# Two attention layers and two feed-forward layers on one core: weights of the routed layer and two contexts are loaded ahead of the iterations, the first keys stored there too, with other stages and orders on all engines

## The chip, the core and the metric

The kernel runs on one core of one Trainium2 chip. The metric is the device time in microseconds (us) of one launch, a median of runs.

## The reference, cut to what matters

For x of shape (16, 128, 256) and a context of the same shape, batch by batch:

```python
x = x + _L0_xattn_ref(_layernorm(x), ctx_2048, ctx_2048)   # 16 heads of 16 columns, causal softmax
x = x + _L0_ffn_ref(_layernorm(x), base_w, base_b, router_w, router_b, lora_A, lora_B)
                                                            # dense 256x256 plus two of 8 rank-16 experts by top-2 gates
x = x + _L1_xattn_ref(_layernorm(x), ctx_2048, ctx_2048, gamma)  # the same on 8 heads over columns: 256x256 scores, no mask
x = x + _L1_ffn_ref(_layernorm(x), w1, w2, gamma)           # rms norm, 8-bit activations, ternary weights, 256 -> 1024 -> 256, gelu
```

All is float32. The kernel keeps that precision in the scores by splitting each query and key into three bf16 parts, stacked along the rows of the array.

## The kernel before

**One batch at a time through a pipeline over t.** Each of the five engines has its own in-order program: `iterations` calls a function per iteration t, `fill` for t = 0 to 7, `body` for t = 8 to 15 (14 and 15 as a hardware loop of one turn) and `drain` from 16 to END - 1 = 45. In it every operation is called once, in an order written out by hand, and works on batch b = t - stage, where the stages are the constants at the top of the file (LOAD_KV = 0, ROWS0 = 2, COPY_MAX0 = 4 ...). Engines count t each for themselves and meet only in semaphores; a stage thus says how an operation stands in its own engine's order and not when it runs. An operation whose wait isn't met holds up all behind it on its engine.

**Attention 0 (names ending in 0).** SP loads the context (`load_kv`). GpSimd splits it into the bf16 parts of K (`k_high`, `k_rest_`, `k_mid`, `k_low`), except batch 0, which VectorE splits in `split_k0`. SP stores them to DRAM (`store_k`) and loads them back re-laid by heads (`load_k0`). ScalarE normalises x (`norm0`, `norm0_high`), GpSimd makes the parts (`q0_rest`, `q0_mid`, `q0_low`), TensorE turns them (`turn_q0`), ScalarE copies them (`copy_q0`), SP stores and loads them (`store_q0`, `load_q0`). TensorE computes the scores a first time (`scores0`, four groups), VectorE takes row maxima and splits them (`maxima0`, `split_max0`, `split_max0_low`), TensorE turns them (`turn_max0`), ScalarE copies them (`copy_max0`), SP writes them into two further rows of the query tile with two transfers of 4 KB (`rows0`). Then TensorE computes the scores transposed and with the maximum taken off (`scores0_t`), ScalarE exponentiates (`exp0`), TensorE multiplies by V (`pv0`), ScalarE copies the sums (`copy_u0`), TensorE turns them (`turn_u0`), VectorE divides and adds (`rz0_`, `a0_`, `x1_`).

**Routed layer.** `stats1_`, `mv1_`, `rstd1_`, `norm1`, `turn_xh1`, `copy_xh1`, `ff` (two float32 products of 392 columns, L1256), then `logits_`, `top_`, `gap_`, `exp2`, the gates, `gated_`, `turn_gated`, `copy_gated`, `lora` (L1273), `moe_out`.

**Attention 1** runs the same way (names ending in 1; `load_k1`, `load_q1`, `rows1`), some five iterations later. **The last layer** (`xn_`, `amax_in`, `round_in`, `quant_in`, `turn_in`, `up`, `gelu`, `amax_hid`, `round_hid`, `quant_hid`, `turn_hid`, `copy_hid`, `down`, `scale_output`, `add_output`) runs in `drain` alone.

**Queues.** All loads and stores of contexts, keys, queries and rows go through SP's queue in program order. x in groups and all weights go through ScalarE's. In `fill` SP's order of an iteration is rows1, load_kv, store_k, load_v1, load_q0, rows0, load_k0, store_q1, load_k1, load_q1, store_q0. `load_q0` and `load_k0` of batch b wait for the last `scores0_t` of batch b - 2, `load_kv` of b for K's split of b - 1 and for `place_v0` of b - 2.

## Time and profile before

| | us |
|---|---|
| median of 3 runs | 413.86 |
| lowest, highest | 408.65, 415.42 |
| the profiled execution | 415.81 |
| its span in the trace | 413.4 |
| granted TensorE clock, mean | 0.93 |

The span is the time between the first and the last instruction of the trace; 2.4 us of the profiled execution lie around it. PE is TensorE's matmuls, PEld its weight loads, DVE VectorE, ACT ScalarE, POOL GpSimd. SPq and ACTq are the queue of an engine (its sequencer), where transfers are issued. A row with DMA in the chain of waits runs from the issue of a transfer to its landing.

### The profile page before, as it was taken

To read this page: it belongs to the slowest core of one execution; us is meant where nothing else is said; L and a number is where in the kernel's file an instruction comes from. 1 tells how busy PE (TensorE), PEld (TensorE's weight loads), DVE (VectorE), ACT (ScalarE), POOL (GpSimd) and SP (SyncE) were. 2 spreads that over 40 slices of the span, in tenths; PEclk is the share of its full clock that TensorE was granted. 3 is DMA by queue.
4 is the path that set the end of the run, shared out by engine and by line. 5 is a ranking of instruction groups with operands and counts; after the bars stand their busy time and mean duration, and the time that the engine had idled before them with its cause. 6 is when DMAs were issued, how large, how long until landed. Compare 5 with 4: busy or idle time off the path is not lost.

```text
span 413.4 us, 9678 instructions
## 1 busy us (share of the span) xinstructions
PE 318.2 (77%) x3010; PEld 192.7 (47%) x3010; DVE 307.9 (74%) x838; ACT 264.4 (64%) x501; POOL 230.9 (56%) x449
## 2 busy tenths in 40 slices
PE   0047366497799899999999999999787578566883
PEld 0024244264465465665655665665443234234453
DVE  6432362759899687889997978897885574999983
ACT  2124153355577488789777876777465347988993
POOL 6257465838585557769656676235424113566534
PEclk9996796888899899999999999999996789999999
DMA  3675774976655738658757577623413400001111
GB/s 101 203 210 131 223 212 105 271 204 168 169 152 172 219 86 237 187 167 225 201 159 212 147 209 193 166 57 92 108 57 94 90 2 1 2 17 36 39 52 63
DMA packets 73137, 56.20 MB, mean 136 GB/s; under 512 B 5376, under 2 KB 62592, under 8 KB 73088
## 3 DMA queue, kind: packets, MB, share of 16 engines
q1 hardware_dynamic: 68896, 50.87, 44.8%
q10 hardware_dynamic: 4192, 4.73, 4.5%
q8 instruction: 24, 0.39, 0.5%
q14 instruction: 25, 0.20, 0.2%
HBM read 36.45 MB, written 18.87 MB: 134 GB/s over the span
## 4 chain that ended last, share of the span: by engine, by line
PE 45%; DMA 16%; DVE 12%; issue 9%; ACT 8%; SPq 6%; POOL 3%; ACTq 0%; POOLq 0%; DVEq 0%
DMA q<-max_t 8%; PE ps_u L1186 6%; PE ps_st L1155 6%; PE ps_s L1140 5%; DMA k<-k_parts 5%; PE ps_ff L1256 4%; PE ps_st L1122 3%; PE ps_st L1126 3%; PE ps_u L1169 3%; DVE max L1801 3%; PE ps_s L1104 2%; PE ps_t L1284 2%; PE ps_s L1108 2%; SPq L616 2%; DMA k_parts<-k_split 2%
## 5 line engine op out<-in xcount | busy, mean ns | idle before, releaser
L1801 DVE TENSOR_REDUCE max<-ps_s 128x2 f32<-128x512 f32 (+1 forms) x192 | 127.1, 685 | 49.0 <-PE ps_s L1108 28.0
L1507 ACT ACTIVATE p<-ps_st 128x512 f32<-128x512 f32 x128 | 71.9, 596 | 23.6 <-PE ps_st L1155 15.6
L1497 ACT ACTIVATE p<-ps_st 128x512 f32<-128x512 f32 x64 | 37.2, 597 | 30.3 <-PE ps_st L1126 29.9
L1140 PE MATMUL ps_s<-k,q 96*128 96x256 bf16 x256 | 51.2, 284 | 5.6 <-DMA k<-k_parts 3.2
L1155 PE MATMUL ps_st<-q,k 98*128 98x256 bf16 x256 | 48.0, 288 | 4.9 <-ACT p L1507 3.1
L1186 PE MATMUL ps_u<-p,v 128*32 128x256 f32 x512 | 39.5, 422 | 3.4 <-POOL v L874 3.4
L1122 PE MATMUL ps_st<-mask_k,ident_bf 128*128 128x512 bf16 x64 | 26.9, 421 | 18.3 <-DMA q<-max_t 17.5
L1155 PEld LDWEIGHTS ps_st<-q,k 98*128 98x128 bf16 x256 | 21.8, 102 | 20.9 <-issue 6.4
L1140 PEld LDWEIGHTS ps_s<-k,q 96*128 96x128 bf16 x256 | 20.3, 100 | 22.8 <-issue 10.9
L923 POOL TENSOR_SCALAR var<-mv 128x1 f32<-128x1 f32 x32 | 7.3, 229 | 41.8 <-DVE mv L1890 34.1
L1284 PE MATMUL ps_t<-ident_bf,q_split 128*128 128x128 bf16 x128 | 12.8, 259 | 21.6 <-POOL q_split L897 21.6
L817 POOL TENSOR_SCALAR k_split<-kv_in 128x1024 bf16<-128x1024 f32 x15 | 15.7, 1049 | 24.2 <-DMA k_parts<-k_split 20.1
L1256 PE MATMUL ps_ff<-wff_sb,xh_t 128*128 128x392 f32 x64 | 27.5, 556 | 2.0 <-DVE w_mean L2048 1.6
L1126 PE MATMUL ps_st<-q,k 98*128 98x128 bf16 x256 | 27.3, 233 | 0.0
L1104 PE MATMUL ps_s<-mask_q,ident_bf 128*128 128x512 bf16 x64 | 25.7, 401 | 1.7 <-DMA k<-k_parts 1.7
L1126 PEld LDWEIGHTS ps_st<-q,k 98*128 98x128 bf16 x256 | 21.7, 105 | 11.1 <-issue 3.5
L1511 ACT ACTIVATE xh<-xs,shift,rstd 128x256 f32<-128x256 f32 x32 | 19.2, 601 | 11.9 <-POOL shift L926 7.8
L1108 PE MATMUL ps_s<-k,q 96*128 96x128 bf16 x256 | 26.0, 226 | 0.0
L1568 ACT COPY q_t<-ps_t 128x1024 bf16<-128x1024 bf16 x16 | 16.1, 1006 | 15.1 <-PE ps_t L1284 15.1
L1169 PE MATMUL ps_u<-p,v 128*32 128x128 f32 x512 | 25.5, 292 | 0.0
L1027 POOL TENSOR_SCALAR amax_c<-amax,rms 128x1 f32<-128x1 f32 x16 | 4.9, 307 | 36.6 <-DVE amax L2203 35.9
L1108 PEld LDWEIGHTS ps_s<-k,q 96*128 96x128 bf16 x256 | 20.7, 101 | 8.7 <-issue 1.4
(147 smaller groups left out, 798.3 us busy)
## 6 DMA issues: line engine op xcount, KB each, us to landing
k_parts<-k_split SPq DMA_DIRECT2D x16, 512.0 KB, 4.1
q<-q_parts SPq DMA_DIRECT2D x32, 256.0 KB, 3.8
k<-k_parts SPq DMA_DIRECT2D x32, 256.0 KB, 3.6
kv_in<-in_kv SPq DMA_DIRECT2D x16, 256.0 KB, 3.7
q_parts<-q_t SPq DMA_DIRECT2D x16, 256.0 KB, 3.7
q<-q_parts SPq DMA_DIRECT2D x32, 128.0 KB, 3.9
k<-k_parts SPq DMA_DIRECT2D x32, 128.0 KB, 3.6
q_parts<-q_split SPq DMA_DIRECT2D x16, 256.0 KB, 2.8
```

Of the source, the lines that this page charges most:

```text
L1104: pe.matmul(out_[:, :], ident_bf[:, :], mask_q[:, :, :].rearrange("p g k -> p (g k)"), start=True, stop=False, skip_group_check=True)
L1108: last = pe.matmul(out_[:, j * P:(j + 1) * P], q0[0:STK, odd, c:c + P], k0[0:STK, odd, c:c + P], start=False, stop=(j == G - 1), skip_grou ...
L1122: pe.matmul(out_[:, :], ident_bf[:, :], mask_k[:, :, :].rearrange("p g k -> p (g k)"), start=True, stop=False, skip_group_check=True)
L1126: last = pe.matmul(out_[:, j * P:(j + 1) * P], k0[0:STM, odd, c:c + P], q0[0:STM, odd, c:c + P], start=False, stop=(j == G - 1), skip_grou ...
L1140: last = pe.matmul(out_[:, f * D:(f + 1) * D], q1[0:STK, odd, h * D + f * P:h * D + (f + 1) * P], k1[0:STK, odd, h * D:(h + 1) * D], start ...
L1155: last = pe.matmul(out_[:, f * D:(f + 1) * D], k1[0:STM, odd, h * D + f * P:h * D + (f + 1) * P], q1[0:STM, odd, h * D:(h + 1) * D], start ...
L1169: last = pe.matmul(ps_u[32 * j:32 * j + 32, g * P:(g + 1) * P], v0[:, odd, h, :], p0[:, g, j * P:(j + 1) * P], start=True, stop=True, skip ...
L1186: last = pe.matmul(ps_u[32 * j:32 * j + 32, g * D:(g + 1) * D], v1[:, f * H1 + h, :], p1[:, h, f * D:(f + 1) * D], start=(f == first), sto ...
L1256: last = pe.matmul(ps_ff[:, 0:NFF], xh1_t[:, f, :], wff_sb[:, f, :], start=(f == 0), stop=(f == FT - 1), skip_group_check=True)
L1497: act.activation(p0[:, g, :], ps_st[bank_of(ST_BANKS, f"s0t{g}")][:, :], ACT.Exp, scale=SCALE).then_inc(exp0_done[g], 1)
L1507: act.activation(p1[:, h, :], ps_st[bank_of(ST_BANKS, f"s1t{h}")][:, :], ACT.Exp, scale=SCALE).then_inc(exp1_done[h], 1)
L1801: dve.tensor_reduce(out_, src, AX.X, ALU.max, negate=True).then_inc(done, 1)
```

## The change

1. **Ahead of the iterations**: SP loads both context 0 and context 1, waits for `split_k0`, and stores the keys of batch 0 (`send_k(0)`). ScalarE's queue issues the third group of x, base_b, w_ff in two transfers, router_b and lora_b. Before, context 1 and keys 0 stood in SP's iteration 1 behind `store_q0` of batch 0, and the weights in ScalarE's iteration 2. The two gammas go to iteration 3. One semaphore for six weights becomes three (`base_b_in`, `w_ff_in`, `lora_in`). Groups 4 and 5 of x and w1, w2 are loaded one iteration later, and the sums over w1 and w2 are taken one later (`W_BATCH` 10 - FF; `weight_sum(0)` at the end of t = 7, `stats0_group(5)` of t = 8, `weight_sum(1)` of t = 9).
2. **Orders in fill**: on TensorE `turn_gated`, `lora` and `turn_q0` stand before `scores0_t`, `ff` and all four `pv0` before `turn_max0`. On SP `load_k0` stands before `rows0`. On ScalarE `copy_max0` follows `exp2` and `copy_u0`, and `copy_gated` and `copy_q0` follow at once, before `exp0`. On GpSimd `k_rest_` and `k_mid` go ahead of `rstd1_`, and `q1_rest` stands between `k_high` and `q0_low`.
3. **Orders in body**: SP's `rows1` is first, before `load_kv`. ScalarE's `norm2` goes before `copy_max0`. Orders of `pv0`, `pv1` and of some DVE operations are exchanged.
4. **Drain and stages**: `xn_` 17 to 16, `rms_` 17 to 18, `quant_in` 20 to 21, `copy_hid` 27 to 28, `down` 28 to 29, `scale_output` 30 to 31, `add_output` 29 to 31, `dequant_in` 20 to 23, `dequant_hid` 27 to 30, END one more. On DVE `copy_hid` stands before `amax_hid`; on TensorE `down` is first and `up` and `turn_hid` go ahead of the last groups.
5. **Waits**: `norm0` and `norm2` wait for `q0_rest` (`q1_rest`) of the batch before, no longer for its `q0_low` (`q1_low`).

```diff
-X_ITERATIONS = {0: 2, 1: 3, 3: 4, 5: 5}
-W_LOADS = {4: 0, 6: 1}
-W_BATCH = 9 - FF
+X_ITERATIONS = {1: 3, 4: 4, 6: 5}
+GAMMAS = 3
+W_LOADS = {5: 0, 7: 1}
+W_BATCH = 10 - FF
...
             load_x(sp, 0)
             load_x(sp, 1)
+            sp.dma_start(kv_in[:, 0, :, :], kv[0]).then_inc(kv0_landed, 16)
+            sp.dma_start(kv_in[:, 1, :, :], kv[1]).then_inc(kv_landed, 16)
+            sp.wait_ge(k_split_step, 4)
+            send_k(0)
             iterations(sp, fill, body, drain)
...
             def fill(t, odd):
-                rows1(t, odd)
                 load_kv(t, odd)
                 store_k(t)
+                rows1(t, odd)
+                load_q0(t, odd)
+                load_k0(t, odd)
+                rows0(t, odd)
+                store_q1(t)
+                load_k1(t, odd)
                 load_v1(t, odd)
-                load_q0(t, odd)
-                rows0(t, odd)
-                load_k0(t, odd)
-                store_q1(t)
-                load_k1(t, odd)
                 load_q1(t, odd)
                 store_q0(t)
...
-                act.wait_ge(q0_split_step, b * 3)
+                if later(b, 1):
+                    act.wait_ge(q0_split_step, b * 3 - 2)
...
             act.activation(warm[:, :], warm[:, :], ACT.Exp)
+            load_x(act, 2)
+            act.dma_start(base_b_all[:, :], base_b.partition_broadcast(P)).then_inc(base_b_in, 16)
+            for f in range(FT):
+                act.dma_start(wff_sb[:, f, :], w_ff[f * P:(f + 1) * P, :]).then_inc(w_ff_in, 16)
+            act.dma_start(router_b_all[:, :], router_b.partition_broadcast(P)).then_inc(w_ff_in, 16)
+            act.dma_start(lora_b_sb[:, :], lora_b).then_inc(lora_in, 16)
             iterations(act, fill, body, drain)
```

TensorE's and ScalarE's orders in `fill` are new throughout; as they stand after the change, cut behind `turn_max0` and `exp0(t, 0)`:

```python
def fill(t, odd):
    scores1_t(t, odd, 6)
    turn_back(t)
    scores1(t, odd, 6)
    scores1(t, odd, 2)
    scores1(t, odd, 0)
    turn_u0(t)
    scores1(t, odd, 1)
    turn_gated(t)
    scores1_t(t, odd, 1)
    scores1(t, odd, 3)
    lora(t)
    pv1(t, 0, 0)
    turn_q0(t)
    scores1(t, odd, 7)
    scores0_t(t, odd, 1)
    scores0_t(t, odd, 2)
    scores1(t, odd, 4)
    scores0(t, odd, 2)
    pv1(t, 1, 0)
    scores0(t, odd, 3)
    scores1_t(t, odd, 2)
    scores0_t(t, odd, 0)
    turn_max1(t)
    scores0_t(t, odd, 3)
    scores0(t, odd, 0)
    turn_xh1(t)
    scores0(t, odd, 1)
    turn_u1(t)
    pv0(t, odd, 1)
    pv1(t, 0, 1)
    ff(t)
    pv0(t, odd, 2)
    pv0(t, odd, 3)
    pv0(t, odd, 0)
...
    turn_max0(t)
...
def fill(t, odd):
    norm2_high(t)
    exp1(t, 0)
    exp1(t, 7)
    norm2(t)
    exp2(t)
    copy_u0(t)
    copy_max0(t)
    copy_gated(t)
    copy_q0(t)
    norm0(t)
    exp1(t, 5)
    exp0(t, 1)
    exp0(t, 2)
    norm1(t)
    copy_max1(t)
    exp0(t, 3)
    exp1(t, 2)
    exp1(t, 4)
    copy_xh1(t)
    norm0_high(t)
    copy_u1(t)
    exp0(t, 0)
```

## Rows read from the trace of the kernel before

**Rows 1.** The page: busy time by engine, and the granted clock in 40 slices.

```profile
PE 318.2 (77%) x3010; PEld 192.7 (47%) x3010; DVE 307.9 (74%) x838; ACT 264.4 (64%) x501; POOL 230.9 (56%) x449
...
PEclk9996796888899899999999999999996789999999
```

**Rows 2.** The page's transfers: tiles, queue, count, KB each, median us to landing.

```profile
k_parts<-k_split SPq DMA_DIRECT2D x16, 512.0 KB, 4.1
...
q_parts<-q_t SPq DMA_DIRECT2D x16, 256.0 KB, 3.7
```

**Rows 3.** Timeline of SP's queue in fill: start, us, queue and line, transfer.

```profile
11.87 0.33 SPq L664 DMA_DIRECT2D q_parts<-q_t  x1
12.24 0.43 SPq L634 DMA_DIRECT2D kv_in<-in_kv  x1
...
30.43 1.23 SPq L728 DMA_DIRECT2D q<-max_t  x2
...
43.43 1.46 SPq L728 DMA_DIRECT2D q<-max_t  x2
...
57.79 1.43 SPq L728 DMA_DIRECT2D q<-max_t  x2
...
74.92 1.28 SPq L728 DMA_DIRECT2D q<-max_t  x2
```

**Rows 4.** The chain that ended last, 0 to 125 us: start, us, what.

```profile
12.79 7.96 DMA k_parts<-k_split
...
21.48 3.45 DMA k<-k_parts
...
31.07 2.70 DMA q<-max_t
...
44.30 5.13 DMA q<-max_t
...
51.37 0.85 PE ps_t L1284 x8
...
58.40 6.85 DMA q<-max_t
...
68.61 1.09 PE ps_ff L1273 x2
...
75.54 6.40 DMA q<-max_t
...
123.80 2.19 DVE w_sum L2040
```

**Rows 5.** Timeline of ACT around one copy_max0 in fill.

```profile
57.51 0.26 ACT L1576 COPY max_t<-ps_t 32x128 bf16<-32x128 bf16 x1 [0.35 <-PE ps_t L1230]
...
57.91 0.20 ACT L1615 ACTIVATE e<-gap 128x1 f32<-128x1 f32 x1
...
58.01 0.57 ACT L1592 COPY u<-ps_u 128x512 f32<-128x512 f32 x1
```

**Rows 6.** Waits: engine and line, for whom, us in total, times, longest.

```profile
POOL k_split L817 <- DMA k_parts<-k_split: 20.1, 5, 7.1
```

**Rows 7.** Windows: us, busy time and count by engine, granted clock, DMA share, GB/s.

```profile
60.00:62.00 2.00, 0.33 (x1) 0.14 (x1) 1.25 (x5) 0.27 (x1) 1.75 (x4) 1.00 1.15 281
...
160.00:180.00 20.00, 19.94 (x216) 11.91 (x215) 16.41 (x51) 16.07 (x34) 13.94 (x24) 1.00 0.70 198
```

**Rows 8.** Timeline of the last layer: two xn, two amax_hid, the last down.

```profile
374.00 0.46 DVE L2195 SCALAR_TENSOR_TENSOR xn<-xs,mv,mlp_gamma_all 128x256 f32<-128x256 f32 x1
...
378.02 0.46 DVE L2195 SCALAR_TENSOR_TENSOR xn<-xs,mv,mlp_gamma_all 128x256 f32<-128x256 f32 x1
...
393.72 1.22 DVE L2221 TENSOR_REDUCE amax<-hid 128x1 f32<-128x1024 f32 x1 [0.44 <-ACT hid L1736]
...
396.64 1.22 DVE L2221 TENSOR_REDUCE amax<-hid 128x1 f32<-128x1024 f32 x1 [0.43 <-ACT hid L1736]
...
408.87 1.05 PE L1434 MATMUL ps_ff<-w_q,hq_t 128*128 128x256 bf16 x8 [0.79 <-DVE hq_t L2258]
```

446 lines of the change are left out of this document (222 added, 224 removed).

## The prediction, made before the changed kernel was run

> **What bounds the kernel now.** I read the page first. TensorE is busiest, 318.2 of 413.4 us, and the slices show where it is not: the granted clock drops in the first quarter and again late, and is at its upper level, 2.4 GHz, for most of the middle [rows 1]. The windows split the span in four. The fill (to about 125 us) has idle engines everywhere; between 60 and 62 us TensorE works 0.33 of 2 us, while the 16 DMA engines are busy throughout [rows 7]. The middle (to about 250 us) is TensorE's: 19.94 of 20 us at full clock [rows 7]. Next comes the end of the attention layers (to 351 us), then the last layer alone, on VectorE and ScalarE.
>
> I then followed the chain of waits through the fill, with SP's queue beside it. It goes round one ring per iteration: `rows0` issues two small transfers, they land, `scores0_t`, `turn_q0`, `pv0`, `lora`, the next `scores0` and `ff` run, the maxima are turned and copied, the next `rows0` issues. `rows0` stands at 30.43, 43.43, 57.79 and 74.92 us: rings of 13.0, 14.4 and 17.1 us [rows 3]. Steady iterations take about 15.6 us of TensorE's work. The transfers of these rings (the second of two) landed in 2.70, 5.13, 6.85 and 6.40 us [rows 4]. They carry 4 KB, so the three long ones waited behind larger ones.
>
> **The change, part by part.** *Keys 0 and context 1 ahead.* Before, `store_k` of batch 0 was issued at 12.79 us, behind `store_q0` and `load_kv` (11.87, 12.24) [rows 3], landed after 7.96 us beside the weights, and its keys 3.45 us after the last issue, so that the first scores could begin at 24.93 [rows 4]. Now the store goes out when VectorE has split (about 7.4 us there, 1 to 2 later if the early loads slow context 0) and has landed before `store_q0`. `store_q0` at 11.87, plus 3.7 [rows 2], plus four issues of 0.6 us, plus 3.45, gives 21.3. I take a start 3.1 us earlier at `rows0` (bounds 1.5 and 4.5: the split late, or all of the difference).
>
> *Landing of `rows0`.* Before, `store_q0`, `load_kv`, `store_k` (1 MB) and 384 KB of `load_q0` are issued in the 5 us ahead of it. Now `turn_q0` doesn't follow `scores0_t` and `copy_q0` follows `copy_max0`, so those stores come behind `rows0`, and about 10 us remain until the next. Against that, `load_k0` (384 KB, two issues) goes ahead of it; those loads are issued once the last `scores0_t` is out, some 4 us before the maxima are copied, so SP is free by then. I take 3.3 us, near the one unhindered row (2.70) and above it for what still overlaps: 1.8, 3.5 and 3.1 less, 8.4 in all. Bounds: nothing (the queues stay full) and 10.3 (2.70 each).
>
> *What leaves the ring.* `turn_q0` (0.85 us at the low clock, five rings) and `lora` (1.09, two rings) [rows 4] run while `rows0` is in flight: 4.3 + 2.2 us. `pv0` of group 1 moves behind the scores to the full clock: 1. Bounds 4 and 9 (the ring has other members where ScalarE was last).
>
> *What enters it.* `copy_max0` now waits for `exp2` (0.20) and `copy_u0` (0.57) and thus for all `pv0`, where before it came ahead of both [rows 5]. With two hand-overs and two more `pv0` groups of about 0.36 that is up to 1.9 per ring; the path through the maxima (1.3 + 0.85 us after the last scores) hides about half. I take 0.9 over five rings: 4.5 (bounds 2 and 9.5).
>
> Sum of the fill: -3.1 - 8.4 - 4.3 - 2.2 - 1.0 + 4.5 = -14.5. Walking the new orders by hand from the start, with row durations, I come to `rows0` at 39 instead of 43.4, 52 instead of 57.8 and 65 instead of 74.9. From t = 5 `copy_gated` stands before `copy_q0`, the attention-1 traffic joins, and 768 KB of x come one iteration later, so I give 2.5 back: **-12**.
>
> *Weight sums.* `weight_sum(0)` stood in VectorE's wait at t = 6 and now ends t = 7; `weight_sum(1)`, 2.19 us on the chain [rows 4], only moves to t = 9; six batches of x statistics go from the end of t = 7 to that of 8. One more sum is exposed: **+2.2** (bounds 0 and 4.5, the statistics too).
>
> *Body.* TensorE has no idle time to give, so the orders bring little. `rows1` goes out ahead of `load_kv` (0.43 us of issue [rows 3]), where its landing was at times the last thing waited for; `norm2` goes before `copy_max0` (0.6 us). The looser waits of `norm0` and `norm2` are free: those norms run behind longer queues. I take **-1** (bounds -3 and +3).
>
> *Drain and last layer.* There VectorE sets an iteration of 4.02 us (`xn_` at 374.00 and 378.02), and from about 385 us ScalarE one of 2.92 (`amax_hid` at 393.72 and 396.64), with 0.43 us of idle VectorE [rows 8]. `xn_` one iteration earlier and `copy_hid` one later take 0.46 and 0.68 us out of the VectorE-bound stretch. The end pays: `copy_hid` of batch 15 must now wait for `down` of 14, which waits for `copy_hid` of 14, all behind `quant_hid` of 15, where before `quant_hid` of 15 was followed by its turn (0.61), its copy (0.68) and its `down` (1.05 [rows 8]). That is 0.68 + 1.05 in place of the turn, +1.2 with the hand-over. Together **+0.2** (bounds -1.5 and +3).
>
> Total: -12 + 2.2 - 1 + 0.2 = -10.6, so the span goes from 413.4 to 402.8 and the profiled execution from 415.81 to 405.2, a ratio of 0.9745. The profiled execution stood 0.5% above the median of 413.86, so against that median the forecast is 403.3; I say **403.5**.
>
> **The clock.** About four of the eight score groups of an iteration run at 1.2 GHz in the rings above (0.85 us each in the timeline, 0.45 at 2.4), behind 4 to 5 us in which TensorE was idle: the slices with 6 and 7 [rows 1]. `turn_gated`, `lora` and `turn_q0` now fall in that gap. My sum keeps the low clock. If the gap were filled well enough, 1.6 us per ring, 8 us over five, would come on top: 395.5. The trace gives no case in which two short bursts held the clock up, so that is a rival of small chance. The Trainium skill (TensorE: Matmul & The Clock Gate, The HAM clock gate) says that activity releases the throttle and idleness restores it; the trace agrees, as the clock falls in every such wait. By it the 395.5 would come if what is now in the gap counts as activity, and the 403.5 if it doesn't.
>
> **The rivals.**
>
> *A. The landing doesn't get shorter (chance 0.22).* In 60 to 62 us the engines were busy at over 100% of the window at 281 GB/s [rows 7], and `load_k0` now adds 384 KB right ahead of `rows0`. For: all queues end in the same transfer engines. Against: the 1 MB of stores is gone from ahead of it. Then -8.4 becomes 0 or -1, the fill about -4.5, and the time 411. The Trainium skill (DMA: Bandwidth & Descriptors, Issuing engines are not separate DMA queues) states that transfers issued by different engines run on the same 16 DMA engines and interleave, and that issuing from several saves issue time alone. By it the early weights slow context 0 and the first term would be its 1.5; no row shows the two loads side by side.
>
> *B. The fill's gain is lost in the body (0.12).* TensorE is full [rows 7], so an earlier start carries through only if batches aren't held by VectorE, which takes both the sum and the statistics in t = 7 to 9. If `norm2` before `copy_max0` costs its 0.6 us in each of some 14 later iterations, 8.4 us go: 412.
>
> *C. The clock stays up (0.08).* 395.5, as above.
>
> *D. Slower: the ring of keys becomes the bound (0.07).* Now TensorE must pass `turn_q0` before `scores0_t`, `turn_q0` of b needs `q0_low` of b, which stands behind `k_high` of b on GpSimd, and that waits until `store_k` of b - 1 has landed. GpSimd waited 20.1 us in 5 times for this, once 7.1 [rows 6]. By my walk the store is issued 8 us after `ff`, lands 4.1 later [rows 2], and GpSimd needs 2 to 3 more (14 to 15 in all); the turn is wanted at 18.4, a ring of 12.8 later and 5.6 on, when `rows0` has landed. From a landing of about 8 us on, the fill's iterations grow. With 8 of landing, 8.6 of GpSimd's work (its longest stretch from one `k_high` to its `k_low`) and 3 of turn, copy and issue they take 19.6 instead of the 17.1 of the longest ring: six give +15, less 3 for the start, +2 from the rest: 428. At half that excess 421, about where "slower" begins. Queued behind on TensorE would be `scores0_t` and all after it.
>
> *E. Nothing moves (0.05)*: the ring is re-formed by ScalarE (`copy_gated` before `copy_q0` waits for a chain of gates of 3 to 4 us), 413.
>
> The forecast itself has 0.46 and the range 397 to 408.
>
> **How the numbers follow.** Faster by over 2% means below 405.6, slower above 422.1, about what a measurement of this kernel can tell from no change (its three runs span 1.6%). Faster: 0.35 of the forecast's 0.46, all of C (0.08), and 0.07 of A and B, where no more than half of their loss comes: 0.50. Slower: 0.05 of D and 0.02 of B at its bounds: 0.07. The same: 0.43. Eight in ten lie between 393, which reaches past C, and 415, past A, B and E, which leaves out D and the tails.
>
> **What would show it.** First `scores0` at 21 to 22.5 us; `rows0` near 27, 39, 52 and 65; the second of its transfers landing in about 3.3 us; `turn_q0` ahead of `scores0_t` with no wait on it for GpSimd; the chain in the fill without `turn_q0` and `lora`; the body at 15.6 us an iteration; weight sums on the chain twice; about 60 us from the last `out_` to the end, as now. Landings of 5 to 7 us mean A, waits of TensorE for `q_split` mean D, waits of `copy_q0` for `turn_gated` mean E.

## The result, and the profile after

The changed kernel takes 416.47 us (median of 20 runs) where the kernel before takes 414.37 (20 runs), a ratio of 1.0088 with a 95% interval of 1.0044 to 1.0131. It is a little slower, where 403.5 was forecast. Ratios here and below compare undisturbed runs only, so they differ a little from the quotient of two medians.

The profiled execution has a span of 414.9 us, 1.5 more than before. The page after, as in [rows 1]:

```profile
PE 323.6 (78%) x3010; PEld 197.7 (48%) x3010; DVE 316.3 (76%) x838; ACT 264.8 (64%) x501; POOL 234.7 (57%) x449
...
PEclk9999787896899999999999999999887688699999
```

TensorE and VectorE do the same instructions in more time (323.6 and 316.3 us instead of 318.2 and 307.9). Marks in the timelines divide the 1.5 us:

| us in the span | before | after | difference |
|---|---|---|---|
| `copy_max0` of b = 0 | 30.1 | 26.6 | -3.5 |
| `copy_max0` of b = 4 | 92.4 | 86.2 | -6.2 |
| `copy_max0` of b = 5 | 108.7 | 105.8 | -2.9 |
| last `out_` (attention layers end) | 351.6 | 348.6 | -3.0 |
| from last `out_` to the end | 61.8 | 66.3 | +4.5 |

`copy_max0` of b = 0 is the copy of the row maxima of batch 0. So a gain is made in the fill, half of it is gone by the sixth batch (b = 5), and the last layer takes more than what is left.

**The start.** The chain of waits and, behind it, SP's queue (the lines to set beside [rows 3, 4]):

```profile
1.63 6.17 DMA kv_in<-in_kv
...
23.65 4.70 DMA k_parts<-k_split
...
30.38 2.88 DMA q<-max_t
```

```profile
26.58 0.26 ACT L1589 COPY max_t<-ps_t 32x128 bf16<-32x128 bf16 x1 [3.19 <-PE ps_t L1239]
...
28.43 0.58 SPq L619 DMA_DIRECT2D k<-k_parts  x1
29.06 0.62 SPq L620 DMA_DIRECT2D k<-k_parts  x1
29.73 0.61 SPq L733 DMA_DIRECT2D q<-max_t  x1
```

Context 0 is issued at 1.63 us, as before, but lands after 6.17 us, before the change after 3.1: `base_b`, `w_ff`, `router_b` and context 1 were issued between 1.4 and 2.9 us and `lora_b` at 4.8 (x[2] went out at 0.9 us before the change too). That they share the transfer engines with it is borne out below, where it lands after 3.2 us without them. Batch 0's keys are therefore stored at 11.01 us, not 7.4. Its maxima are copied at 26.58 all the same, 3.5 us earlier than before. But SP stands at `load_k0` of batch 1, which waits for a store issued at 23.65 and landed at 28.4, and `rows0` is queued behind it: it goes out at 29.73, 0.7 us earlier than before. The chain of waits runs from the late context 0 through VectorE's and GpSimd's work on the parts to this store.

**The rings.** `rows0` stands at 29.73, 42.79, 58.16, 72.68, 87.05 and 106.06 us. The chain from 54 us on, at the third of them and after:

```profile
57.96 1.08 DVE pick L1954
...
59.86 0.49 PE ps_t L1275
...
60.37 0.27 ACT gated_t L1635
...
60.69 1.22 PE ps_ff L1284 x2
61.91 0.85 PE ps_t L1295 x8
62.77 0.58 PE ps_st L1131
```

The gates are computed (`pick`), turned and copied (`gated_t`), then `lora` and `turn_q0` run, and only then the first `scores0_t` (62.77), 4.6 us after `rows0` was issued. The landing is not on this chain, but it ends within 0.1 us of it: the second transfer was issued at 58.8 and took 3.9 us. In the fourth ring `turn_q0` is done first and TensorE waits 1.2 us for the landing.

The clock takes its part of each ring. In the second ring the scores begin at 47.42 us, 2.1 earlier than before. The score groups (a product with the mask, then four with the keys) after the change, and the first rows of the same ring before it:

```profile
47.42 0.61 PE ps_st L1131
...
51.87 0.43 PE ps_st L1131
...
52.72 0.38 PE ps_s L1113
```

```profile
49.48 0.61 PE ps_st L1122
...
52.69 0.32 PE ps_st L1122
```

After the change the first rows at the upper level come at about the same time as before, and more groups have run at the lower one. In rings one to four, 23 of 32 groups start at the lower level (7, 7, 5 and 4 of eight), before 10 (4, 2, 2 and 2). At 0.85 us a group instead of 0.45 that is an estimate of up to 5 us. Three other profiles with the same fill have 18 (fill_only), 21 (body_pe) and 25 (body_act).

At the fifth ring it is a queue again:

```profile
74.27 3.09 DMA q_parts<-q_split
...
81.02 4.66 DMA k_parts<-k_split
...
87.65 7.07 DMA q<-max_t
```

`load_q1` waits for the store of batch 0's second queries, `store_q0` and `store_k` stand behind it, `load_k0` behind the landing of that, and the 4 KB of `rows0` then take 7.07 us. Before the change that landing took 1.8 us. It is where 3.3 of the 6.2 us go.

**The windows**, for [rows 7]:

```profile
60.00:62.00 2.00, 1.65 (x6) 0.98 (x7) 1.22 (x5) 0.27 (x1) 0.23 (x1) 0.50 0.69 100
160.00:180.00 20.00, 19.24 (x212) 12.69 (x210) 16.69 (x46) 17.76 (x34) 13.58 (x23) 1.00 0.67 182
```

The gap is filled now (1.65 of 2 us instead of 0.33), but at a granted clock of 0.50, the lower level. In the middle TensorE is no longer full: 19.24 of 20 us. Its waits there, in 140 to 330 us (for what, us in total, times, longest):

```profile
PE ps_st L1164 <- DMA q<-max_t: 2.9, 5, 1.2
PE ps_st L1131 <- DMA q<-max_t: 2.3, 4, 1.2
```

Nine waits for landings of maxima, 5.2 us; the kernel before has two, 0.9 us together, in the same stretch.

**The last layer** (beside [rows 8]). First its start, then a stretch from 372 us and one from 387 us:

```profile
349.85 1.87 PE L1418 MATMUL ps_s<-w_q,xq_t 128*128 128x512 bf16 x4 [1.25 <-ACT hid L1744]
...
353.65 1.87 PE L1418 MATMUL ps_s<-w_q,xq_t 128*128 128x512 bf16 x4 [1.72 <-ACT hid L1744]
```

```profile
372.31 0.72 POOL L1071 TENSOR_TENSOR xs<-y,xs 128x256 f32<-128x256 f32 x1
...
372.50 1.08 DVE L2263 TENSOR_SCALAR hq<-hr 128x1024 bf16<-128x1024 f32 x1
```

```profile
387.33 0.68 DVE L2263 TENSOR_SCALAR hq<-hr 128x1024 bf16<-128x1024 f32 x1
387.49 0.58 POOL L1053 TENSOR_SCALAR amax_c<-amax 128x1 f32<-128x1 f32 x1 [1.33 <-DVE amax L2235]
...
388.04 0.72 POOL L1071 TENSOR_TENSOR xs<-y,xs 128x256 f32<-128x256 f32 x1
...
388.11 0.16 DVE L2254 RECIPROCAL qscale<-amax_c 128x1 f32<-128x1 f32 x1
388.19 0.72 DVE L2247 TENSOR_SCALAR xq<-xr 128x256 bf16<-128x256 f32 x1
...
388.31 1.24 ACT L1754 ACTIVATE hr<-hid,round_all,qscale 128x1024 f32<-128x1024 f32 x1 [0.23 <-DVE qscale L2254]
```

At the start three `up`s, of the second to the fourth batch, take 1.87 us at the lower clock, where those of the kernel before take 1.02, and the first three iterations take 3.8, 3.8 and 5.3 us instead of 2.9, 3.4 and 4.0. Later, instructions of VectorE and GpSimd that touch take longer. VectorE's `quant_hid` takes 1.08 us instead of 0.68 beside GpSimd's `add_output` (the rows at 372 us), and `xq` 0.72 or 0.75 instead of 0.28. From 387 us on `keep_amax_hid` on GpSimd (one number a partition, 0.21 to 0.23 us in all but one batch of the kernel before) takes 0.58 beside `quant_hid` in four batches, and two iterations take 3.24 us instead of 2.92. From the first `amax_hid` to the last it is 53.8 us, before 49.7, and this is where it goes:

| us between `amax_hid` of | before | after | copy_between | up_late | two_lines |
|---|---|---|---|---|---|
| b = 0 and 3 | 10.3 | 12.9 | 11.4 | 10.3 | 9.7 |
| b = 3 and 5 | 8.0 | 8.0 | 8.0 | 8.0 | 8.0 |
| b = 5 and 9 | 13.8 | 15.5 | 14.4 | 15.5 | 14.4 |
| b = 9 and 15 | 17.6 | 17.4 | 17.4 | 17.1 | 17.5 |

The last three columns are experiments that come below. The loss lies in the first three iterations (2.6 us) and between b = 5 and 9 (1.8). The two iterations of 3.24 us cost nothing in the end, since the four behind them take 2.60 to 2.89.

### The profile page after: what moved, and what is told of

The parts are those of the page before. It is cut to its first block, busy times and chain, and to the rows that moved or that the text cites. A ratio compares the mean times of both kernels' runs of the same rounds, so it can differ in the third digit from the quotient of the medians.

```text
span 414.9 us, 9679 instructions
## 1 busy us (share of the span) xinstructions
PE 323.6 (78%) x3010; PEld 197.7 (48%) x3010; DVE 316.3 (76%) x838; ACT 264.8 (64%) x501; POOL 234.7 (57%) x449
## 4 chain that ended last, share of the span: by engine, by line
PE 26%; DMA 18%; issue 16%; DVE 13%; POOL 12%; SPq 10%; ACT 3%; POOLq 0%; ACTq 0%; DVEq 0%
DMA q<-max_t 10%; DVE max L1815 4%; PE ps_u L1195 4%; DMA k_parts<-k_split 4%; SPq L620 3%; PE ps_st L1164 3%; PE ps_s L1149 3%; PE ps_st L1131 3%; POOL xs L1071 3%; PE ps_st L1135 3%; SPq L619 2%; DMA q_parts<-q_t 2%; SPq L742 2%; PE ps_s L1418 2%; DMA kv_in<-in_kv 1%
## 5 line engine op out<-in xcount | busy, mean ns | idle before, releaser
L1195 PE MATMUL ps_u<-p,v 128*32 128x256 f32 x512 | 38.3, 423 | 3.6 <-POOL v L883 3.6
L1131 PE MATMUL ps_st<-mask_k,ident_bf 128*128 128x512 bf16 x64 | 28.6, 447 | 13.7 <-DMA q<-max_t 13.6
L932 POOL TENSOR_SCALAR var<-mv 128x1 f32<-128x1 f32 x32 | 9.4, 294 | 51.0 <-DVE mv L1904 34.9
L1164 PEld LDWEIGHTS ps_st<-q,k 98*128 98x128 bf16 x256 | 21.8, 102 | 21.4 <-DMA q<-max_t 7.7
L1149 PEld LDWEIGHTS ps_s<-k,q 96*128 96x128 bf16 x256 | 19.8, 99 | 24.7 <-issue 16.1
L1295 PE MATMUL ps_t<-ident_bf,q_split 128*128 128x128 bf16 x128 | 11.5, 241 | 23.0 <-POOL q_split L906 23.0
L1135 PE MATMUL ps_st<-q,k 98*128 98x128 bf16 x256 | 28.7, 242 | 0.0
L1135 PEld LDWEIGHTS ps_st<-q,k 98*128 98x128 bf16 x256 | 22.9, 110 | 11.4 <-issue 4.7
L1117 PE MATMUL ps_s<-k,q 96*128 96x128 bf16 x256 | 28.3, 240 | 0.0
L1113 PE MATMUL ps_s<-mask_q,ident_bf 128*128 128x512 bf16 x64 | 28.3, 442 | 0.0
L1117 PEld LDWEIGHTS ps_s<-k,q 96*128 96x128 bf16 x256 | 22.8, 109 | 10.6 <-issue 4.4
L1522 ACT ACTIVATE q_split<-xs,shift,rstd 128x256 bf16<-128x256 f32 (+1 forms) x32 | 22.6, 706 | 7.6 <-POOL shift L935 7.5
L1265 PE MATMUL ps_ff<-wff_sb,xh_t 128*128 128x392 f32 x64 | 26.6, 541 | 0.8 <-ACT xh_t L1621 0.5
L1418 PE MATMUL ps_s<-w_q,xq_t 128*128 128x512 bf16 x64 | 18.9, 423 | 10.4 <-ACT hid L1744 10.4
```

The source lines that it names most:

```text
L1113: pe.matmul(out_[:, :], ident_bf[:, :], mask_q[:, :, :].rearrange("p g k -> p (g k)"), start=True, stop=False, skip_group_check=True)
L1117: last = pe.matmul(out_[:, j * P:(j + 1) * P], q0[0:STK, odd, c:c + P], k0[0:STK, odd, c:c + P], start=False, stop=(j == G - 1), skip_grou ...
L1131: pe.matmul(out_[:, :], ident_bf[:, :], mask_k[:, :, :].rearrange("p g k -> p (g k)"), start=True, stop=False, skip_group_check=True)
L1135: last = pe.matmul(out_[:, j * P:(j + 1) * P], k0[0:STM, odd, c:c + P], q0[0:STM, odd, c:c + P], start=False, stop=(j == G - 1), skip_grou ...
L1149: last = pe.matmul(out_[:, f * D:(f + 1) * D], q1[0:STK, odd, h * D + f * P:h * D + (f + 1) * P], k1[0:STK, odd, h * D:(h + 1) * D], start ...
L1164: last = pe.matmul(out_[:, f * D:(f + 1) * D], k1[0:STM, odd, h * D + f * P:h * D + (f + 1) * P], q1[0:STM, odd, h * D:(h + 1) * D], start ...
```

## The experiments

My theory after the two profiles: the early loads eat the lead of the first keys; the fill's new orders still gain; the last layer's orders lose about 4 us, by the slow `up` and by the meeting of VectorE and GpSimd; the body loses, by `norm2` in front of `copy_max0` (rival B). The rival theory: one thing is at fault, the start, and the rest is scatter. Kernels of one group ran side by side with the kernel before, so that ratios, not medians, are to be compared across groups. The medians are of 6 to 12 runs, those of before of 11 to 29.

| kernel | median | before | ratio [95%] |
|---|---|---|---|
| u_drain | 414.37 | 413.07 | 1.0005 [0.9956, 1.0054] |
| u_body | 415.18 | 413.07 | 1.0022 [0.9981, 1.0062] |
| u_fill | 420.84 | 413.07 | 1.0138 [1.0071, 1.0205] |
| u_weights | 416.44 | 413.07 | 0.9971 [0.9901, 1.0040] |
| clear_start | 416.83 | 415.19 | 1.0031 [0.9989, 1.0072] |
| all_three | 410.66 | 415.19 | 0.9849 [0.9792, 0.9906] |
| copy_between | 416.64 | 415.19 | 0.9978 [0.9933, 1.0022] |
| up_late | 416.01 | 415.19 | 1.0034 [0.9990, 1.0078] |
| fill_only | 409.63 | 412.21 | 0.9901 [0.9851, 0.9951] |
| rows_first | 406.64 | 412.21 | 0.9892 [0.9847, 0.9937] |
| max_first | 417.82 | 412.21 | 1.0169 [1.0109, 1.0229] |
| lead_alone | 412.41 | 412.21 | 0.9978 [0.9930, 1.0026] |
| body_act | 409.40 | 414.31 | 0.9883 [0.9838, 0.9927] |
| body_dve | 409.52 | 414.31 | 0.9909 [0.9872, 0.9946] |
| body_pe | 414.50 | 414.31 | 0.9972 [0.9920, 1.0024] |
| body_sp_pool | 415.08 | 414.31 | none given |
| two_lines | 416.50 | 413.60 | 1.0108 [1.0056, 1.0160] |
| weights_t1 | 407.67 | 413.60 | 0.9831 [0.9771, 0.9890] |

### Undoing one part at a time

**u_drain**: the stages and orders of `drain` as before.

```
-COPY_HID = 28        +COPY_HID = 27
-DOWN = 29            +DOWN = 28
 (and the other stages, and def drain of all five engines)
```

> The changed kernel, with the stages of the last layer and all five drain orders of the kernel before; lead-in, fill and body stay changed. Theory (the new order of the last layer costs 4 to 5 us): from the last out_ to the end it takes 62 us again instead of 66, and the time falls by about 4.5 us against the changed kernel, to a ratio of 0.998 against before. Rival (the last layer only pays for work that the attention part got rid of, 3 us there): the end falls by 4.5, the attention part grows by 3, ratio 1.005.

From the first `amax_hid` to the last it is 49.7 us again, and the span is 410.4. In the eleven profiles with the drain of before it is 49.6 to 49.7 us, in the six with the change's drain 53.8 to 53.9: the last layer does cost 4.2 us. The time is 0.8% below that of the change, with intervals that just overlap.

**u_body**: `def body` of all engines as before.

> The changed kernel with the body orders of before on all engines; the places of the weight work stay. Theory (the body lost 3 us of the fill's 6 through its new orders): 3 us faster than the changed kernel, ratio 1.002. Rival (it lost them through the statistics and the sums that moved into t = 8 and 9): no difference, 1.009.

0.7% below the change, again with intervals that just overlap. The profile alone would have said less (span 413.2 against 414.9).

**u_fill**: the fill's orders, and the iterations of the x and weight loads, as before; the start, the body and the drain are the change's.

> The changed kernel, with the fill orders of before on all engines and before's times for x, w1, w2 and the sums over weights; the lead-in (early context 1, keys 0 and weights), body and drain stay changed. Theory (the new fill orders are worth 5 us at t = 7 and the body gives half of it back): 2 to 3 us slower than the changed kernel, ratio 1.015. Rival (what the fill gains is lost in the body, whatever it was): no difference, 1.009.

Slower than the change, by 0.5% with overlapping intervals; the span is 2.6 us longer (417.5 against 414.9). The new fill orders seem to be worth something; nothing shows that they cost.

**fill_only** undoes drain and body together:

> The changed kernel with the body's orders, the last layer's stages and the last layer's orders of the kernel before; the start with its early loads and the fill's orders are those of the change. It differs from all_three by the start alone. If the early loads cost 3 us at the start that nothing gives back, it lies 2 to 4 us above all_three, at 412.5 to 414.5. If the chain of the fill swallows the start, it lies within 1 us of all_three, 410 to 411.5.

1.9% below the change, intervals apart, and 1% below the kernel before. Against all_three (below) it lies 0.5% higher, about 2 us, with intervals that overlap, so which of its two outcomes holds is not decided. The accounts of the parts add up to within 0.4% (0.8 + 0.7). fill_only also differs from u_drain by the body alone (1.0%) and from u_body by the drain alone (1.2%), with intervals apart in both. The six kernels with the new fill that have neither the new drain nor TensorE's, SP's or GpSimd's new body lie at 0.983 to 0.991, all others with the new fill at 0.997 to 1.017.

### The start

**u_weights** and **clear_start** take the early loads out of context 0's way:

```
+                if t == 2:
+                    act.dma_start(base_b_all[:, :], ...).then_inc(base_b_in, 16)
+                    ... w_ff, router_b, lora_b
-            load_x(act, 2)                      # clear_start only; back in t = 0
             sp.wait_ge(k_split_step, 4)
             send_k(0)
+            sp.dma_start(kv_in[:, 1, :, :], kv[1])...   # clear_start only; was ahead of the wait
```

> The changed kernel, but base_b, w_ff, router_b and lora_b are issued at the end of ScalarE's iteration 2 again instead of ahead of the iterations. Theory (they share the transfer engines with context 0, which landed after 6.2 us instead of 3.0): context 0 lands in 3 to 4 us, rows0 of batch 0 stands at 27 us instead of 29.7, and 2 us of it last to the end, ratio 1.004. Rival (later waits take it up): rows0 of batch 0 earlier, the end the same, 1.009.

> The changed kernel with its start emptied of everything but x[0], x[1] and kv[0]: the loads of base_b, w_ff, router_b and lora_b stand at the end of ScalarE's iteration t=2, x[2] again in t=0, and kv[1] is issued by SP behind send_k(0). All orders are those of the change. Theory 1 (the early loads share the 16 DMA engines with kv[0], whose landing went from about 3.0 us before to 6.17 us after, and so ate the lead of the first keys): kv[0] lands after 3.0 to 3.5 us, k_split of head group 0 starts at 4.7 to 5.2 us instead of 7.8, store_k(0) is issued at 7.5 to 8.2 us instead of 11.0, the first row maxima are copied at 24 to 25.5 us instead of 26.6, and the time is 3 to 6 us below the changed kernel's, 411 to 413. Rival 2 (the start has slack: the first scores wait for x and the queries, not for the keys): store_k(0) moves, copy_max0(0) stays within 0.7 us of 26.6, time 415 to 417. Rival 3 (kv[1] comes too late behind send_k): iteration 1 starts 2 to 3 us later, and the time is 417 or more.

In u_weights context 0 lands after 3.71 us, the keys of batch 0 are stored at 8.64 and `rows0` goes out at 27.72, 2.0 us earlier than in the change; `copy_max0` of b = 15 is 4.5 us earlier. The ratio, 0.9971, is 1.2% below the change's and lower than the 1.004 expected, but it rests on four runs. So the early weights cost the start 2 us.

In clear_start too the mechanism is there: context 0 lands after 3.2 us, `k_split` starts at 4.90 us, `store_k` of batch 0 goes at 7.53. Yet `copy_max0` of batch 0 is at 28.5, two later than in the change. The chain:

```profile
11.72 3.96 DMA q_parts<-q_t
...
17.88 4.33 DMA k<-k_parts
...
27.04 1.09 DVE max_split L1845
```

```profile
26.93 1.15 POOL L842 TENSOR_TENSOR k_rest<-kv_in,k_split 128x512 f32<-128x512 f32 x1
```

With the keys out of the way, the store of the queries sets the scores, and that lands later (3.96 us; 3.0 in the change, where the weights had gone; here they are issued at about the same time). And one subtraction of 128x16 numbers on VectorE takes 1.09 us instead of 0.17, because GpSimd's `k_rest` started 0.11 us earlier. `copy_max0` of batch 1 is 4.0 us earlier than in the change (38.6), though the ten other profiles with the change's start and fill have it at 40.1 to 42.4; at b = 6 it is 4.5. Then it is lost: b = 6 to 15 takes 153.3 us instead of 149.4. Rival 2's time, without rival 2's cause.

**lead_alone** is the kernel before with nothing but the keys of batch 0 pulled ahead:

```
             load_x(sp, 1)
+            sp.dma_start(kv_in[:, 0, :, :], kv[0]).then_inc(kv0_landed, 16)
+            sp.wait_ge(k_split_step, 4)
+            send_k(0)
+            sp.dma_start(kv_in[:, 1, :, :], kv[1]).then_inc(kv_landed, 16)
             iterations(sp, fill, body, drain)
```

> The kernel before with the first keys alone hoisted: SP issues kv[0] behind x[1], waits for k_split, stores the keys of iteration 0, issues kv[1], and only then enters the iterations. The weights' loads and all orders are those of before. Theory 1 (the store of the first keys, 12.8 us before, sets the first scores): it is issued at 7.5 to 8 us, the first scores and copy_max0(0) come 3 to 4 us earlier (26 to 27 instead of 30.1), and 1.5 to 3 us of it reach the end: 411 to 413. Rival 2 (the first scores are held by the queries of b=0 or by the orders on the engines): copy_max0(0) moves by less than 1 us, time unchanged, 413.5 to 415.5. Rival 3 (later iterations of the fill are paced by the landings of the row maxima and give the lead back): copy_max0(0) is 3 us earlier, copy_max0(4) less than 1 us, time 413 to 415.

```profile
11.92 4.32 DMA q_parts<-q_t
...
18.43 6.42 DMA k<-k_parts
...
30.13 0.26 ACT max_t L1583
```

The store goes 5.1 us earlier (7.74 instead of 12.79), and the maxima are copied at 30.13, exactly as before. The last load of the keys goes out 3.05 us earlier and takes 2.97 us longer than that of [rows 4] (6.42 instead of 3.45): the weights, the queries and the keys are all still in flight between 12 and 25 us, and from 20 to 25 the transfer engines are busy throughout (the DMA share of that window is 1.07). Rival 2. The chain of waits had shown which transfer came last, not that the others were done sooner.

**weights_t1** puts the four weights where ScalarE is done with t = 1, on top of all_three (below):

> all_three with the loads of base_b, w_ff, router_b and lora_b at the end of ScalarE's iteration t=1 instead of t=2. In clear_start ScalarE is done with its work of t=1 at about 8 us, and the DMA engines are 0.63 busy from 8 to 12 us and 0.66 from 12 to 16. If these 0.9 MB fit there, the queries' store (issued at 11.7 us) lands as before after 4 us, the DMA share from 20 to 24 us falls from 1.04 to below 0.8, copy_max0(0) comes at 26 to 27.5 instead of 28.5 us, and the time is 0 to 2 us below all_three (ratio 0.980 to 0.987). If they stand in front of the stores of keys and queries, copy_max0(0) comes at 28.5 to 31 us, and the ratio is 0.987 to 0.995.

They go out at 6.5 to 9.0 us. `copy_max0` of batch 0 stays at 28.4 us, so the expected step is missed; the ratio of 0.9831, within what its theory said, is the lowest of all, not distinguishable from all_three's 0.9849.

### The body

**max_first** is clear_start with one line moved, and tests rival B's cause. The waits it takes away, in clear_start:

```profile
234.00 0.23 PE L1239 MATMUL ps_t<-ident_bf,max_split 128*32 128x128 bf16 x1
...
234.52 0.81 ACT L1522 ACTIVATE q_split<-xs,shift,rstd 128x512 bf16<-128x512 f32 x1 [1.31 <-POOL shift L935]
...
235.73 0.24 ACT L1589 COPY max_t<-ps_t 32x128 bf16<-32x128 bf16 x1
```

```
                 copy_u0(t)
-                norm2(t)
                 copy_max0(t)
+                norm2(t)
```

> clear_start with one line moved: in ScalarE's body order copy_max0 stands ahead of norm2 again, as in the kernel before. In the profiles with the changed body order copy_max0 is issued 0.8 us (b = 6, 7, 9), 2.3 us (b = 10, 11) and 1.5 us (b = 12, 13) after the transpose that it reads, because norm2 ahead of it waits for GpSimd's rstd2; with the body orders of before the waits are 0 to 0.4 us, but one of 1.0. Theory 1 (these waits are on the path from one iteration to the next): they vanish, the time from copy_max0 of b=6 to b=15 falls from 153.3 us (clear_start) to 145 to 149, and the time by 4 to 6 us, to 411 to 413. Rival 2 (the iteration has that much slack, or norm2, now later, delays the second head group by as much): the waits vanish, b=6 to b=15 stays at 149 to 154 and the time within 2 us of clear_start, 415 to 418.

The waits vanish up to b = 11, and in the profile b = 6 to 15 falls from 153.3 to 149.5 us. The kernel is not faster: 1.0169, where clear_start has 1.0031, though from three runs. TensorE still waits 6.5 us in 8 times for landings of maxima. So the waits before `copy_max0` don't explain the body's cost, and my theory of it fell.

So the body was taken apart by engine. Each of the next four is fill_only with `def body` of one engine (SP and GpSimd together) from the change; body_pe also has the change's unit orders of the body.

> fill_only (ratio to the kernel before 0.990) with ScalarE's body order of the change alone: norm2 and norm2_high ahead of and behind copy_max0, copy_q0 ahead of norm0_high, exp0(0) behind copy_max1. Theory (the cost of the body, about 0.7%, comes from what stands in front of copy_max0): copy_max0 waits 0.8 to 2.3 us for rstd2 as in the changed kernel, and the ratio is 0.995 to 1.000. Rival (another engine's order costs it; what max_first says): the waits are there or shorter, and the ratio stays within 0.986 to 0.994.

> fill_only with VectorE's body order of the change alone: stats2 and mv2 stand four to six instructions later, mv2 directly ahead of split_max0, so GpSimd's rstd2 and ScalarE's norm2 start later. Theory (the late mv2 delays norm2, the queries of the second head group and their store, which SP waits for ahead of the next keys): store_q1 is issued 1 to 2 us later in each body iteration, the time from copy_max0 of b=6 to b=15 rises from 144.3 us to 147 or more, and the ratio is 0.995 or more. Rival: b=6 to b=15 within 1.5 us of 144.3 and a ratio of 0.986 to 0.993.

> fill_only with TensorE's body order of the change alone (turn_back behind scores1(2), the pv0 pieces in the order 2, 1, 0, 3, pv1(1, 1) last). A steady iteration is bound by the chain of scores and maxima rather than by these pieces, which only trade places; expected ratio 0.987 to 0.993, b=6 to b=15 within 1 us of 144.3. If it is TensorE's order that costs the 0.7%, the ratio is 0.996 or more and waits of VectorE for ps_ut or ps_t grow.

> fill_only with SP's and GpSimd's body orders of the change. SP issues load_v1 and load_kv behind rows1 instead of load_kv first: where rows1 waits for copy_max1, the next kv and the next keys are issued later. Theory (SP's queue costs it): kv is issued 1 to 4 us later against copy_max0 in the body, k_parts too, b=6 to b=15 rises by 3 us or more, ratio 0.996 or more. Rival (kv has a whole iteration to land): later issue, no change in the periods, ratio 0.986 to 0.993.

ScalarE's and VectorE's orders cost nothing that the time shows (0.9883, 0.9909; fill_only 0.9901), although b = 6 to 15 takes 148.8 and 147.9 us instead of 144.2. In body_act `copy_max0` mostly doesn't wait as its theory needs (0.8 us at b = 10 and 11, where the change has 2.3), so VectorE's late `mv2` has its part in those waits. TensorE's order comes out 0.7% above fill_only, with intervals that overlap. SP's and GpSimd's have no interval: five of the six runs lie between 413.8 and 422.3, one at 407.5. The expectations of body_pe and body_sp_pool put the period at 144.3 and 147 or more; it is 153.9 and 153.1, but both profiles are of the slowest of their runs. So the times point to these two and don't show it. The waits say the same. TensorE's waits for landings of maxima in 140 to 330 us add up to 0.3 us in fill_only, 0.8 in body_act, 1.0 in body_dve, 2.1 in body_pe, 3.2 in body_sp_pool; and over all profiles, the kernels with the body of the change (max_first's with its one line moved) have 5.1 to 7.9 us of them, and those with the body of before, or with ScalarE's or VectorE's order alone changed, 0.3 to 1.8. In SP's body order `load_v1` and `load_kv` now stand between `rows1` and `store_k`. Whether that is the fault, or another of its moves or of GpSimd's, was not tried.

What can come with such a wait is seen in body_pe. In the chain SP's issue of `kv_in`, just ahead of `rows1`, takes 2.09 us (usually 0.35), and the rows land late:

```profile
203.64 2.09 SPq L636
...
206.54 2.84 DMA q<-max_t
```

```profile
204.00:208.00 4.00, 2.81 (x28) 1.41 (x25) 3.75 (x9) 2.12 (x6) 3.41 (x6) 1.00 0.73 198
208.00:212.00 4.00, 2.95 (x28) 1.19 (x32) 1.41 (x7) 1.35 (x4) 3.01 (x6) 0.85 0.78 233
212.00:216.00 4.00, 4.00 (x36) 2.60 (x29) 2.29 (x10) 2.51 (x5) 3.16 (x5) 0.72 0.74 194
```

TensorE is idle for 2.2 of the 8 us from 204 on, in two gaps of 1.34 and 0.90 us, of which the second waits for these rows. The granted clock is 0.85 in the window from 208 us and 0.72 in the next, in which TensorE is busy throughout, and the iteration takes 20.2 us, where most take 15.5 to 17. The gaps are paid again in the clock.

### The last layer

**copy_between** and **up_late** each move one line of the changed kernel, the first in VectorE's drain, the second in TensorE's:

```
-                copy_hid(t)
                 amax_hid(t)
+                copy_hid(t)
...
-                up(t)
                 scores0_t(t, odd, 2)
...
                 pv1(t, 1, 1)
+                up(t)
```

> The changed kernel with one line moved: in VectorE's drain order copy_hid stands behind amax_hid instead of ahead of it, so that it lies between amax_hid and quant_hid as in the kernel before. Theory 1 (keep_amax_hid on GpSimd takes 0.58 us instead of 0.21 because it runs beside VectorE's quant_hid, and scale_hid waits for it): keep_amax_hid falls to 0.21 to 0.3 us, the period of the last layer from 385 us on falls from 3.24 to 2.9 to 3.0 us, and the end comes 1 to 2 us earlier: 414 to 416. Rival 2 (the period is set by ScalarE's and VectorE's own work, whatever stands between): keep_amax_hid falls, the period stays above 3.15 us, time 416 to 417.5. Rival 3 (copy_hid now delays the way from amax_hid to hr): period above 3.3 us, time above 418.

> The changed kernel with one line moved: in TensorE's drain order up(t) stands behind pv1(t, 1, 1), near the end of the iteration as before, instead of ahead of scores0_t(t, 2). Theory 1 (up itself isn't late by its place but slow, 1.87 us for its four matmuls at the low clock instead of 1.02): the first three periods of the last layer stay at 3.7 to 3.8 us and the time at 415.5 to 417.5. Rival 2 (its place makes ScalarE's gelu wait): the first three periods fall to 3.0 us and the time by 2 to 3 us, to 413 to 414.5.

Both effects are there. In copy_between `keep_amax_hid` runs beside `hq_t`, a copy out of PSUM, takes 0.21 us, and from 384 us on the iteration is 2.9 us, though `quant_hid` now takes 0.98 beside `add_output`. By the table above that stretch (b = 9 to 15) is no shorter for it. What copy_between gains lies between b = 5 and 9, 1.1 us, where `quant_hid` now takes 0.68 to 0.72 us instead of up to 1.08 and `xq` 0.28 instead of 0.75, and in the first three iterations, 1.5 us, where one `up` fewer ran at the lower clock:

```profile
391.19 0.68 DVE L2272 TENSOR_SCALAR hq_t<-ps_st 128x1024 bf16<-128x1024 bf16 x1
391.35 0.21 POOL L1053 TENSOR_SCALAR amax_c<-amax 128x1 f32<-128x1 f32 x1 [1.00 <-DVE amax L2235]
391.52 0.73 POOL L1071 TENSOR_TENSOR xs<-y,xs 128x256 f32<-128x256 f32 x1
...
391.82 0.98 DVE L2263 TENSOR_SCALAR hq<-hr 128x1024 bf16<-128x1024 f32 x1
```

In up_late no `up` takes longer than 1.03 us and the first iterations take 2.9, 3.4 and 4.0 us, as before: rival 2's periods, by way of the clock, which theory 1 had thought indifferent to the place. The second and third `up`:

```profile
356.24 1.02 PE L1418 MATMUL ps_s<-w_q,xq_t 128*128 128x512 bf16 x4 [0.26 <-ACT hid L1744]
...
358.71 1.02 PE L1418 MATMUL ps_s<-w_q,xq_t 128*128 128x512 bf16 x4 [1.33 <-ACT hid L1744]
```

**two_lines** has both:

> The changed kernel with both one-line moves of the last layer: copy_hid behind amax_hid on VectorE and up(t) behind pv1(t, 1, 1) on TensorE. From the first amax_hid to the last it took 53.8 us in the changed kernel, 51.3 with the first move, 50.9 with the second, 49.7 in the kernel before and in u_drain. If the two are separate costs and together the whole, it takes 49 to 50.5 us here, and the time is that of u_drain, ratio 0.997 to 1.004. If they share one cost, it stays at 50.9 to 51.5.

First to last `amax_hid` is 49.7 us, the whole 4.1 us back. So the two lines are enough for the last layer's part of the profile, though a stretch of 0.6 us is gained at its start and another of as much stays lost between b = 5 and 9. The time does not confirm it: 1.0108, no less than the change's 1.0088, although the profiled execution, the fastest of its six, has a span of 409.8. Of the three, copy_between has a ratio below the change's by 1.1%, up_late one lower by 0.5% with intervals that overlap. two_lines lies 1.3% above copy_between, intervals apart, with a last layer that is 1.6 us shorter; a difference of 1% between two of these ratios is thus weaker evidence than the intervals say. Whether the scatter of the executions (8 us between the lowest and the highest of two_lines, 13 for the change) hides the gain, or the old order of the whole drain helps the attention iterations that still run in it (which u_drain undoes and two_lines doesn't), stays open.

### What beats both

**all_three** is clear_start with the body and the drain of before; **rows_first** moves `rows0` ahead of `load_k0` in SP's fill, on top of it.

> The start of clear_start, the new orders of the fill, and the body's orders and the last layer's stages and orders of the kernel before. If the parts add up as their own runs say (last layer back: -4 us in the profiled spans; body back: -1 to -2; start emptied: -3 to -6), the time is 405 to 409, 1 to 2% below the kernel before. If the attention part is held by the chain that passes from one iteration to the next and not by the fill, what the start gains is given back in the body, and the time is 410 to 413, the same as before.

> all_three with one line moved: in SP's fill order rows0 stands ahead of load_k0, as in the kernel before. In all_three the rows of b=4, issued at 85.27 us right behind the keys (83.32), landed after 6.71 us, and copy_max0 of b=5 came 21.3 us after that of b=4. Theory 1 (the two 1 KB-packet loads of the keys just ahead of the rows in the same queue make them late): that landing falls to 3 to 4.5 us, the period of b=4 to 5 falls to 18 to 19, and the time by 1.5 to 3 us, to 408 to 409. Rival 2 (the keys, now behind the wait for the row maxima, come as much later and set the start of the second pass of scores): period 20 to 22, time 410 to 412. Rival 3 (the first fill iterations suffer: load_k0 waits for copy_max0 there): time 413 or more.

all_three is 1.5% below the kernel before, as the sum of the parts said (1 to 2%). In rows_first the landing is no longer on the chain at batch 4, but the store of the keys takes its place there (8.22 us), and the ring of b = 4 to 5 stays at 21.2 us: rival 2. The ratio is the same within the intervals. The clean start (all_three against fill_only) is worth 0.5%, which the intervals don't separate from nothing.

## Why the prediction was wrong

Two steps failed: the sum of the fill, -12 where -2.9 to -6.2 came, and the term of the last layer, +0.2 where +4.5 came.

**Start, -3.1 at `rows0`: -0.7.** The first scores came at 21.1 us, inside the 21 to 22.5 foretold, but by another way: the keys' store at 11.01 and not at 7.4, the queries' store landing in 3.0 us. (The terms written there add up to 21.4, not 21.3.) For a slowed context 0 the prediction had 1 to 2 us, and its landing of 6.17 instead of 3.1 put the store 3.6 us late. The Trainium skill (DMA: Bandwidth & Descriptors, Issuing engines are not separate DMA queues), which the prediction named under rival A, agrees with the rows in this: context 0 landed in 6.17 us with the other loads beside it, in 3.2 in clear_start without them. By it the prediction made the term 1.5; it was 0.7. u_weights gives the price, 2.0 us at `rows0`. It reaches `rows0` through SP: the walk put `rows0` out when the maxima were copied, and it stood 3 us behind `load_k0` of the next batch, whose keys were late by the same loads.

**Landings, -8.4.** The three landings that the term was made of went from 5.13, 6.85 and 6.40 us to 3.97, 3.9 and 3.6: 6.9 of the 8.4 us. That part was nearly right. But the fifth went from 1.8 to 7.07, which gives 5.2 back, and in the third ring the landing was no longer alone at the end.

**Leaves and enters the ring, -4.3 -2.2 -1 +4.5.** `turn_q0` did leave the first two rings, and they took 13.1 and 15.4 us all the same, before 13.0 and 14.4. What ran in its place were score groups at the lower clock: 23 of 32 in four rings, before 10, up to 5 us by the estimate above. With "My sum keeps the low clock" the prediction put this term at nothing, and its one rival on the clock, C, had it higher. In the third ring the gates stood beside the landing: with `lora` and `turn_q0` ahead of `scores0_t`, TensorE can't begin the scores until the gates are through. They were through 2.5 us after `rows0` was issued, and with `lora` and `turn_q0` (2.07 us) behind them they ended level with the landing. That is the place of rival E, at 0.05. In the fourth the two were hidden behind the landing, as the walk had it. What enters was 1.2 us at b = 2 and 3 and 0.6 at b = 4, before 0.1, 0.1 and 1.0, and so less than the 4.5.

**Fill in all, -12.** `rows0` was foretold at 27, 39, 52 and 65 and came at 29.73, 42.79, 58.16 and 72.68. At b = 4 6.2 us had been gained, at b = 5 2.9.

**Weight sums and body, +2.2 -1.** In the profile, nothing (last `out_` 3.0 earlier, as at b = 5). In the runs, the body's orders cost 0.7 to 1.0%, 3 to 4 us, about the bound of +3. "TensorE has no idle time to give" was true, and that was the reason why late landings there could only cost. The moves of `rows1` and `norm2` were weighed one by one. That `norm2` is the cause, as rival B had it, was refuted by max_first; the waits point to the orders of TensorE and of SP with GpSimd, and which move does it stays open.

**Drain and last layer, +0.2: +4.5.** The term was sized by instructions moved between two engines' budgets. The iterations of 4.02 us that were to get shorter still took 4.02 (b = 3 to 5), and the end, put at +1.2, cost 0.4. Missing were two things that no count of instructions shows: the clock at which `up` runs (2.6 us in the first three iterations), and which GpSimd instruction meets which VectorE instruction (1.8 us between b = 5 and 9). In the kernel before `copy_hid` lies between `amax_hid` and `quant_hid`; it was taken for 0.68 us of work to be moved away, and its place decides how `quant_hid` and `xq` meet `add_output` and `keep_amax_hid`.

**The sum.** -3.0 + 4.5 = +1.5, where -10.6 was written. Had only the fill been mis-sized, the result would have been about 412, the place of A, B or E, though none of them was the cause in the main. The range ended at 415 because the last layer's bound was +3 and no rival had its place there.

## What to carry to other kernels

A step pulled ahead of its queue gains only if the transfers beside it get out of its way as well: lead_alone moved a store by 5 us and its consumer by nothing. A wait that is taken out of TensorE's way is no gain by its full length if the work behind it then runs longer at the lower clock: count the groups at either level before and after. Before counting an edit as free, list for each instruction on GpSimd which VectorE instruction will run beside it after the edit. And judge the parts of a change by undoing them one at a time: here the start and the fill together were worth 1%, and the body and the drain cost 1.9%.

## What the runs showed of the hardware

- GpSimd and VectorE hold each other up. In the last layer 128x1 on GpSimd took 0.21 us alone or beside a copy from PSUM, 0.58 beside `quant_hid`; `xq` on VectorE took 0.28 or 0.72, `quant_hid` 0.68 or 0.98; in the fill `max_split` took 0.17 or 1.09. The Trainium skill (SBUF — State Buffer, Who interferes with whom) says that the two share a pair of ports as an exclusive lock, for which whoever starts first holds it to its end, and that `tensor_scalar` can take it and operations with two inputs in SBUF do. By that rule each would take what is left of the other's instruction plus its own time: 0.73, 0.85, 1.11 and 1.21 us. Measured are 0.58, 0.72, 0.98 and 1.09, so the rows agree but for 0.12 to 0.15 us less in each.
- One SP issue of a 256 KB load, usually 0.35 us, took 2.09, in front of a transfer of 4 KB that TensorE then waited 0.90 us for.
- Two gaps of TensorE of 1.34 and 0.90 us in body_pe lie in and before a window of 4 us at a granted clock of 0.85, and one at 0.72 follows.
- The same four matmuls of 128x512 (`up`) took 1.87 us in one order of TensorE's drain and 1.02 in another.
